# Another written order in which four engines take the steps of attention and of the recurrence

## The reference, cut to what matters

```
x = x + ln(L0_attn(ln(x)))   # 16 heads, causal window of 128 keys, a pooled "remote" attention, a sigmoid gate that mixes both
x = x + ln(L0_ffn(ln(x)))    # ternary weights, 256 -> 1024 -> 256, gelu
x = x + ln(L1_attn(ln(x)))   # rwkv: s = exp(w)*s + k v^T along the tokens, o = r (s + bonus), group norm, projection
x = x + ln(L1_ffn(ln(x)))    # 16 experts, 4 of them per token, plus one that all tokens use
```

## Time and profile before

| | us |
|---|---|
| median of 3 runs | 2192.03 (2191.49 to 2195.28) |
| the profiled execution, its own time | 2189.07 |
| its span, first to last instruction | 2187.2 |
| PE busy | 1806.0 (83%) |
| DVE busy | 1533.3 (70%) |
| ACT busy | 863.3 (39%) |
| POOL busy | 708.0 (32%) |

### The profile page before, as it was taken

One profiled execution on the slowest core, in us unless ns is written; L12 is line 12 of the kernel. 1 busy time (PEld: TensorE's weight loads), 2 busy tenths in 40 slices (PEclk: granted clock), 3 DMA queues, 4 the chain that ended last, 5 costly groups with the idle time before them and its releaser, 6 DMA issues. The chain is left out here.

```text
span 2187.2 us, 30601 instructions
## 1 busy us (share of the span) xinstructions
PE 1806.0 (83%) x10670; PEld 1160.2 (53%) x10766; DVE 1533.3 (70%) x3312; ACT 863.3 (39%) x1846; POOL 708.0 (32%) x643
## 2 busy tenths in 40 slices
PE   4878998998899899889989988998666654499977
PEld 2544555465455445545545555454444443499953
DVE  2345696698669668866975896697679855577746
ACT  2343353443345333424534443343421223367733
POOL 0000141043114203401420250043038873467641
PEclk9589999999999999999999999999877665699989
DMA  4000000000000000000000000000113234676666
GB/s 143 1 1 10 1 1 10 10 1 1 20 1 1 11 10 1 1 20 0 1 10 10 1 1 20 1 1 1 39 43 105 95 124 158 200 247 201 191 218 266
DMA packets 83416, 119.13 MB, mean 54 GB/s; under 512 B 12666, under 2 KB 70078, under 8 KB 83137
## 3 DMA queue, kind: packets, MB, share of 16 engines
q1 hardware_dynamic: 67088, 79.43, 11.5%
q0 software_dynamic: 13056, 35.68, 4.4%
q10 hardware_dynamic: 3120, 2.06, 0.3%
HBM read 67.43 MB, written 51.79 MB: 55 GB/s over the span
## 5 line engine op out<-in xcount | busy, mean ns | idle before, releaser
L681 DVE TENSOR_TENSOR_SCAN s_buf<-r_work,kvb 128x512 f32<-128x512 f32 x256 | 363.5, 1422 | 0.0
L866 POOL TENSOR_TENSOR p_buf<-s_buf,r_work 128x512 f32<-128x512 f32 x128 | 152.3, 1190 | 458.4 <-DVE s_buf L681 448.6
L956 ACT ACTIVATE probs<-bank_s,nmx 128x256 f32<-128x256 f32 (+1 forms) x512 | 186.9, 452 | 94.1 <-DVE nmx L541 92.6
L866 POOL TENSOR_TENSOR r_work<-s_buf,r_work 128x512 f32<-128x512 f32 x128 | 158.1, 1237 | 171.8 <-DVE s_buf L681 171.5
L974 ACT ACTIVATE pt<-bank_s 128x1024 f32<-128x1024 f32 (+1 forms) x128 | 117.6, 918 | 226.5 <-PE bank_s L1260 226.5
L821 POOL TENSOR_TENSOR rstd<-vare,mhalf 128x4 f32<-128x4 f32 x48 | 48.4, 1008 | 482.8 <-DVE vare L475 482.8
L670 DVE TENSOR_TENSOR kvb<-r_work,bank 128x512 f32<-128x512 f32 x256 | 174.4, 681 | 12.5 <-PE bank L1383 4.4
L1958 POOL DMA_INDIRECT y_rows<-w_in_ys,m_y_idx x144 | 141.8, 985 | 83.1 <-ACT w_in_ys L2046 47.7
L541 DVE TENSOR_REDUCE nmx<-bank_s 128x4 f32<-128x1024 f32 (+1 forms) x128 | 137.6, 1075 | 41.7 <-PE bank_s L1210 40.9
L1382 PE MATMUL bank<-v_hi,sel_v 128*128 128x512 f32 x256 | 129.7, 506 | 20.0 <-DVE kvb L670 13.9
L1210 PE MATMUL bank_s<-kT,qT 32*128 32x256 f32 (+1 forms) x1024 | 138.5, 390 | 0.0
(11 more groups left out here) (405 smaller groups left out, 4173.9 us busy)
## 6 DMA issues: line engine op xcount, KB each, us to landing
m_xs<-x_rows SPq DMA_DIRECT2D x144, 144.0 KB
w_lo<-y_rows SPq DMA_DIRECT2D x4, 2048.0 KB, 22.0
w_hi<-y_rows SPq DMA_DIRECT2D x4, 2048.0 KB, 23.8
w_in_ys<-in_w SPq DMA_DIRECT2D x17, 256.0 KB, 4.0
x_new<-in_x SPq DMA_DIRECT2D x8, 512.0 KB, 4.0
x_after_rwkv<-x_b SPq DMA_DIRECT2D x8, 512.0 KB, 2.9
m_x_all<-x_after_rwkv SPq DMA_DIRECT2D x8, 512.0 KB, 4.5
out<-m_x_all SPq DMA_DIRECT2D x8, 512.0 KB, 3.5
```

Source lines behind the costliest of these rows:

```text
L681: V.tensor_tensor_scan(s_buf[:, n % 2, 1:S + 1], dec[:, n // HD, :], kvb[:, n % 2, :], 0.0, ALU.mult, ALU.add).then_inc(sem["state"], 1)
L866: G.tensor_tensor(p_slot(n), s_buf[:, n % 2, 0:S], rf[:, n // HD, :], ALU.mult).then_inc(sem["rs"], 1)
L956: ins = A(probs[:, n % 2, x, h * w:h * w + w], score_banks[n % 2][:, x, h * w:h * w + w], ACT.Exp, bias=nmx[:, n, 2 * x + h:2 * x + h + 1])
```

## The change

Only the four strings of `ORDER` change. No instruction is added, removed or resized; `ORDER_END` stays.

```diff
 ORDER = dict(
-    tensor="aaarrarrrrrrararrarrraararraararrarrarararrrraararararrraarrarararrraararaaraaarrrrrraarrrrraaaaarraaaaraaraaaaa",
-    vector="ararrrarrarrraararrrrraarraarararrarararraarrarararrarraarrararraarraraarrarararaarrrrarraararraaaaraaraaaaaraa",
-    scalar="aarrrrrraarrarrraraaarrraraararrrrarrrrrararrraarraaraaraaarrrraaarraaaaaraarararrarrarrrarrraaaarraaaaaaarraa",
-    gpsimd="arrrrrarrarrrarrrrrraraarrarararrarrrarraararrarraaraaaaraaaraarrraaararraraaaaaarraaraaaarraarrrrarraraararaa",
+    tensor="aaarrrrrarrrararrararrarararaarrarrararrarrarararararrraararararrraararrrraaararrrarrrrrraaraarraaaaaaaraaaraaaa",
+    vector="arrrrrraaaarrrarararrrrararaararrararararraarrarararrarraarararrarraarararrraaaarrrarrrrrrrraaaaaaaaraaraaraaaaa",
+    scalar="arararrrarrrrarararaaaaraarraarrarrarrraraaaraaaraarrrrrrraarrrraaarrrrrarrrarraarararaaararaararararrrraaaaararaaa",
+    gpsimd="aarrarrrrrrarrrraaraaraaarrarrraaaraaaraarrrrrrrarararrarrarrarrrarrararaaaaaaaaaraaaarrrrraaaaarrraaraaarraaraar",
 )
```

More of the change, by code:

```diff
@@ L83 @@
 ORDER = dict(
-    tensor="aaarrarrrrrrararrarrraararraararrarrarararrraararararrraarrarararrraararaaraaarrrrrraarrrrraaaaarraaaaraaraaaaa",
-    vector="ararrrarrarrraararrrrraarraarararrarararraarrarararrarraarrararraarraraarrarararaarrrrarraararraaaaraaraaaaaraa",
-    scalar="aarrrrrraarrarrraraaarrraraararrrrarrrrrararrraarraaraaraaarrrraaarraaaaaraarararrarrarrrarrrraaaarraaaaaaarraa",
-    gpsimd="arrrrrarrarrrarrrrrraraarrarararrrarrrarraararrarraaraaaaraaaraarrraaararraraaaaaarraaraaaarraarrrrarraraararaa",
+    tensor="aaarrrrrarrrararrararrarararaarrarrararrarrarararararrraararararrraararrrraaaararrrarrrrraraarraaaaaaaraaaraaaa",
+    vector="arrrrrraaaarrrarararrrrararaararrararraraarrrarararrarraarararrarraarararrraaaarrrarrrrrrrraaaaaaaaraaraaraaaaa",
+    scalar="arararrrarrrrarararaaaaraarraarrarrarrraraaraaaraaarrrrrrraarrrraaarrrrrarrrarraarararaaararaararrrraaaaararaaa",
+    gpsimd="aarrarrrrrrarrrraaraaraaarrarrraaaraaaraarrrrrrrarararrarrarrarrrarrrararaaaaaaaaraaaarrrrraaaaarrraraaarraraar",
 )
```

## The result

| | before | after |
|---|---|---|
| median of 6 runs, us | 2190.93 (2181.23 to 2195.28) | 2217.43 (2212.88 to 2226.46) |
| ratio, 95% interval | | 1.0133 (1.0106 to 1.0159) |
| profiled execution, its span | 2189.07, 2187.2 | 2217.52, 2215.7 |
| mean granted clock over the span | 0.906 | 0.892 |

A forecast was written before the change was run, and what follows sets the result against it. No engine is full over a period: DVE's waits count among the scans, the chain of steps in head and tail. 0 + 4.7 - 3.7 = +1.0 us a period, +7 in seven: 2196.1 profiled, 2199 beside the median; range 2181 to 2210.

The forecast's parts named there:

- head: Start of each period: moving the pooled sum behind the mixes costs nothing; taken as 0, bounds 0 to +0.5 us.
- start, to the second *turn_o: First scans: product ahead of p(4), other shifts and waits make the second turn_o 2.5 us late; bounds +1.0 to +3.5.
- from there to step 33's addition: PE sets the pace to the last scores, 1.1 late; four scans in one run then make step 33's addition 4.7 late.
- tail: Step 33 to next L626: earlier Newton rounds 0.7, wait2 moved 0.8, o_back out of the ffn 2.2; 3.7 us gained.
- POOL's next instruction goes ahead of the waiting scan: Among the scans: p(4) runs before scan 5, which takes 2.1 us more than alone; net +1.2 a period.
- The rival that built on this: A waiting DVE instruction goes ahead of POOL's next one: -0.2 us a period, 2190.6, no change; chance 0.22.
- the lateness of the first part is not kept: Rival: scans regain the start's lateness, or it is under 1.5; -1.5 us a period, 2181.5; chance 0.22.
- The 0.4 for *gate: End of scans: POOL's last differences hold gate, so step 33 starts 0.4 us later; bounds 0 to 0.5.
- (a): Tail: o_var starts right behind mix and Newton rounds end earlier, so DVE takes out sooner; 0.7 us gained.
- The clock: Rival: the half-clock stretch before turn2 moves into the ffn; 1.65 us a period, +12 more, 2211; chance 0.08.
- 0.6 for the spreads ahead of *local2* to *local4: Among the scans: fewer spreads ahead of these PE steps make DVE wait twice, 0.3 us each.
- 0.5 back for *remote: Among the scans: DVE's remote comes 0.5 us earlier, because PE no longer spreads ahead of it.

The follow-up runs named there:

- t_product: `s_tail` with only POOL's product moved from behind p(14) to ahead of p(4): 2174.18 us, ratio 0.9939.
- s_tail: The kernel before, with the new order only from the last turn_o on (the tail): 2167.22 us, ratio 0.9908.
- p_pe_start: The kernel after, with PE's string alone back in the old order up to the second quad: 2210.68 us, ratio 1.0103.
- t_pe_start: `s_tail` with PE's string alone in the new order from the head to the second quad: 2233.87 us, ratio 1.0215.
- f_tail_fill: `s_tail` with four useless 128x512 multiplications added to PE's lat_out: 2165.21 us, ratio 0.9907.

## Why the prediction was off, step by step

| step | forecast | measured, order alone | half clock |
|---|---|---|---|
| head | 0 | 0 | -1.2 |
| start, to the second *turn_o* | +2.5 | +1.1 at equal half clock | +4.3 |
| from there to step 33's addition | +2.2 | +1.33 | +0.6 |
| tail | -3.7 | -3.53 | +2.2 |
| sum | +1.0 | -1.1 | +5.9 |

The third column is read where the half clock is equal (start) or off the chain (end, tail); the fourth is the rest of the measured change. The rest fits the price of a stretch: 11.2 us more among the first scans, at 1.2 for 3.41, make 3.9. That the kernel became slower, as forecast, is luck: by the third column the order alone is faster, and what made the kernel slower stands in the fourth.

- **Head.** DVE lost nothing, as said. It even came 1.7 earlier in five periods: there *rturn* starts 12.5 after L626 and not 14.2, since the short half-clock stretch that before had 7.4 after L626 is not there.
- **The product and p(4).** The step that POOL's next instruction goes ahead of the waiting scan failed: in `t_product`, and in after's period from 1197.20, the scan goes first. This is what the Trainium skill, SBUF — State Buffer, section "Who interferes with whom", gives for the shared port pair (whoever issues first has it for the whole instruction), and these traces agree, with scans that had waited 0.97 and 1.94. The row that decided it, is of another kind: in front of its p stands an indirect DMA. That instruction, in before; then the last two scans of after's period from 795.60, and POOL beside them:

```profile
1693.76 0.96 POOL L882 DMA_INDIRECT x_rows<-work,kT  x1 [0.30 <-issue]
...
933.61 3.14 DVE L681 TENSOR_TENSOR_SCAN s_buf<-r_work,kvb 128x512 f32<-128x512 f32 x2
...
934.03 1.64 POOL L828 TENSOR_TENSOR work<-work 128x256 f32<-128x256 f32 x1
935.63 3.23 POOL L866 TENSOR_TENSOR r_work<-s_buf,r_work 128x512 f32<-128x512 f32 x2
```

Scan 31 ends at 936.75, 1.08 after the difference (935.67), and the two p's behind the difference take 3.23 together: p(30) waited for the scan. In all 14 traces, wherever a scan meets a TENSOR_TENSOR on POOL with another queued right behind (177 places, waits of 0.07 to 1.94), the scan goes ahead of the next. Beside an indirect DMA alone it takes 1.21 to 1.22 in all 180 places: it does not wait for one. The p of the earlier trace rows followed the scan's start by 0.35 and overtook it; why that is possible is open. The rival that built on this was right in its mechanism, but its price was too low: by it the product costs 0.4 net, and in before's order it costs 2.4 to 2.7, with scan 6 held as well. In after's order *scores0* stands between *remote* and scan 5, so part of the product runs beside that; the whole start costs 1.1 there.
- **Start.** The estimate of 2.5 was too large: 1.1 (1.9 at the longer stretches). At a half clock of 3.41 the scans take 1.4 more than in `s_tail` (28.0 against 26.6), and DVE's waits 0.2 less. In after itself the second *turn_o* comes 4.7 late in the period from 795.60, 107.06 after L626 against 102.31; in the period from 1197.20 it comes at 102.90. By the forecast's own condition, a first part under 1.5, this was the case of the rival "the lateness of the first part is not kept". By the order alone, 1.1 + 1.33 - 3.53 = -1.1 a period, the kernel would be at about 2181.4 by the profiled execution, 2184 beside the median, within that rival's reach; this is a sum, and no run shows it.
- **End.** 1.33 against 2.2. PE took 24.79 from the second *turn_o* to the last scores, as forecast, though the forecast's own parts, 26.4 - 0.6 - 0.6, make 25.2 and not its 24.9. From the last maximum to the end of p(31) it was 11.36 against 11.65. The 0.4 for *gate* did not arise. Before, *gate* ran alone; in after it met the end of p(30), ended 0.09 behind that, and DVE waited for PE's sum all the same:

```profile
923.13 0.22 DVE L581 TENSOR_TENSOR small<-small 128x64 f32<-128x64 f32 x1
...
937.59 0.30 DVE L581 TENSOR_TENSOR small<-small 128x64 f32<-128x64 f32 x1
940.04 0.69 DVE L687 TENSOR_TENSOR r_work<-r_work,bank 128x512 f32<-128x512 f32 x1 [2.15 <-PE bank L1398]
```

- **Tail.** Right in all three parts, as `s_tail` shows; in after itself (a) is lost to the half clock on *o_tok*, dummies and transposes: addition to *out* takes 12.1 to 13.8 there and not 10.75.
- **The clock.** This is the step that failed. The forecast gave it 0.08, knew one stretch, in front of *turn2*, and asked only whether that would move into the ffn, for 1.65. That stretch went, and none came into the ffn. What came was 11.2 us more half clock among the first scans and 7.3 on the tail's chain, together +7.1, with -1.2 in the head. The forecast had read both causes as waits. It put 4.3 of lateness at the end of the scans and did not ask what PE does meanwhile: PE idles, 3.02. And of PE's moved steps among the first scans it priced only waits, 0.6 for the spreads ahead of *local2* to *local4* and 0.5 back for *remote*, and not the clock. Where half clock lies also decides what it costs: the stretch in front of *turn2* cost nothing, since *resid1*'s addition to the first up product takes 8.67 in before, with it, and 8.67 in `s_tail`, without.

Open is which of PE's moved steps makes the start's stretch long: `p_pe_start` and `t_pe_start` move them together. So is what sets its length in a single period.

## What to carry to other kernels

An order that moves work and waits about on PE can move its clock too, as it did here: ask for each wait that is added, and for each of PE's steps that moves, what the granted clock does in the next 20 us (the longest stretch here), and read it in short windows before the chain is summed. Cut a reordering into its parts and time each: here a tail worth 24 us lay inside a change that cost 26. Dummies meant to keep the clock up have a price when the operand behind them is ready first, so compare their last end with it: here half of them did as well, 1.2 us a period faster.

## What was not expected of the hardware

- The clock fell while PE was busy. In after it fell at 848.0 though PE was busy 7.14 of the 8 us before, with the narrow multiplications of *lat_out* among them; and the clock stayed at half for 17 us while PE was busy for 16.37.
- With the same order of work the stretch among the first scans is 3.41 or 13.65 us in turn (`s_tail`), and the two periods together take 382.3; with 0.86 us of dummies added to each (`f_tail_fill`) the stretches are 3.41 and 6.83 and the two take 382.2. What was added was given back by a shorter stretch, so a change of under 1 us in a period need not show in the time. This is one execution of each; the medians are 2167.22 and 2165.21.
- A scan that had started up to 0.65 us before a p behind an indirect DMA was held by that p in all 84 places of the 14 traces; from 0.66 us on the scan held the p, in all 32.
- The part ahead of the first L626, whose work is the same in the nine kernels without added or removed multiplications, took 195.1 to 205.0 us in their profiled executions. Single executions of one kernel therefore say little below 0.5%.
